# Last token tile turned between the value products, layer 1 in whole tiles, and a last batch normalised and stored tile by tile

## The chip, the core and the metric

The kernel runs on one core of one Trainium2 chip. A core has TensorE (matrix products into PSUM), VectorE, ScalarE, GpSimd and SyncE (SP), which issues most of the transfers. The metric is the device time of one execution in microseconds.

## What is computed

Eight batches of 512 tokens with 256 features go through one attention block with a layer norm, a second layer norm of the sum with the input, a feed-forward part of three layers with ternary weights, and a last layer norm:

```python
# attention: 16 heads of 16, softmax over keys, then multiplied by triu
p = softmax(q @ k.T / sqrt(512)) * triu
x1 = layernorm(x + p @ v) * gamma + beta
x2 = layernorm(x + x1)
# feed-forward, hidden size 1024
h = silu((x2 @ w1) * s1) * ((x2 @ w2) * s2)
h = gelu((h @ h1) * s1h)
h = gelu((h @ h2) * s2h)
out = layernorm(x2 + (h @ w3) * s3)
```

All inputs and outputs are float32.

## The kernel before, in words

The order of each engine's work is written out by hand, one instruction stream per engine, with counting semaphores between them. `after(engine, s, b, n, count)` makes an engine wait until semaphore s has had n signals for each earlier batch and `count` in this one. A loop runs over the batches; in each come the attention of the batch, the head of its feed-forward part (together with the projections of the next batch's q, k and v), and the feed-forward part.

Tokens are in four tiles of 128 (QT = 4), features in two (DT = 2), the hidden size in eight (HT = 8). VectorE normalises one token tile for each group of four heads: `first_norm` and `second_norm`. The power -0.5 of the variance is computed by GpSimd (`rstd`), so each norm goes from VectorE to GpSimd and back. The normalised x2 (tile `X`) is turned by TensorE (`turn_x2`, a transpose by 128 x 128 blocks), in two parts: part 0 is the token tiles 0 to 2 (384 tokens, PSUM banks 4 and 5), part 1 is token tile 3 (128 tokens, bank 0). Each part is then taken by ScalarE into a rounded `X2hi` (`take_x2_hi`), and VectorE computes the rest into `X2lo` (`split_x2`), so that a product of layer 1 is one with the high and one with the low part, both at the rate of the rounded type.

Layer 1 has for each hidden tile m a gate product (`which` 0) and an up product (`which` 1), each of 2 (feature tiles) x 2 (high, low) instructions. `bank1` gives their PSUM bank. ScalarE computes the gate (L639), VectorE the product `hidA_full` (L861) and its rounded part `hidA_hi` (L865), GpSimd the rest `hidA_lo` (`low_part`, L487). Hidden tiles 0 and 1 are computed by `first_layer` (L1173) in two pieces of 384 and 128 tokens, so that they can begin before part 1 is turned; tiles 2 to 7 are computed in `feed_forward` (L1078) over 512 tokens at once. Layer 2 begins on TensorE right behind layer 1 and takes `hidA_lo` tile by tile.

Between the two turns TensorE does work of the next batch: the k projections (L909) and the value products (`project_v`, L926, 16 instructions for the four token tiles). In the last batch there is no next one, and `keep_warm` puts filler products there (L972), whose result is not used. In the other batches the first scores of the next batch are computed inside layers 2 and 3 (L964), from stacks that SP loads from a scratch tensor once GpSimd's `qk_lo` (L507) has been stored.

At the end of a batch VectorE takes y tile by tile (`add_y`: L810, L812, L814), and `last_norm` computes the four aggregates, one add of epsilon, GpSimd one power over four columns (`rstd_last`), and VectorE four normalised tiles into `OUT`, which SP stores with one transfer of 512 KB (L446, in the last batch L468). The order of the head on TensorE before:

```python
turn_x2(b, 0, last)
if not last:
    project(b + 1, range(DT, 2 * DT))
    project_v(b + 1, range(QT))
else:
    keep_warm(7, 20)
first_layer(b, last, 0, 0)
turn_x2(b, 1, last)
first_layer(b, last, 1, 0)
first_layer(b, last, 0, 1)
first_layer(b, last, 1, 1)
```

There is a second, `general`, branch of the feed-forward part for weights that the rounded type doesn't hold; with these inputs it isn't taken.

Of the kernel before, what the change touches and what calls it, by code (L numbers as in the profile page):

```python
# [10 lines left out]
ALU = mybir.AluOpType  # L11
# [42 lines left out]
def build_program(nc, x, xT, wqT, wkT, wvT, bqk, bv, gamma, beta, w1T, w2T, h1T, h2T, scales,  # L54
# [101 lines left out]
    with ExitStack() as ctx:  # L156
# [82 lines left out]

        def bank1(m, which):  # L240

            return 4 + (2 * m + 2 + which) % 4

# [4 lines left out]
        def bank_y(t):  # L248

            return 4 + (t + 2) % 4  # L250
# [42 lines left out]
        def _(sp):  # L293
# [171 lines left out]
            with sp.Else():  # L465
                from_first_feed_forward(False)
            sp.wait_ge(out_ready, QT * B)
            sp.dma_start(out[(B - 1) * S:B * S, :].rearrange("(t p) d -> p t d", p=P), OUT[:]).then_inc(out_stored, 16)  # L468
            sp.wait_ge(out_stored, 16 * B)
            sp.wait_ge(rows_stored, 4 * 16 * B)  # L470
# [4 lines left out]
        def _(pool):  # L475
# [69 lines left out]
            def body(b, first, last):  # L545
                after(pool, probs_ready, b, STEPS, 0)
                after(pool, range_known, b, 1, 1)
                nc.gpsimd.memset(GRANT[:, 1:2], 0.0)
                unbounded = pool.value_load(UNBOUNDED[0:1, 0:1], min_val=0, max_val=1)
                with pool.If(unbounded):  # L550
                    attention(b, first, False)
                with pool.Else():
                    attention(b, first, True)
                if not last:
                    split_qk(b + 1, range(0, 1))
                rstd(b, QT - 1, 0)
                rstd(b, QT - 1, 1)
                if not last:
                    after(pool, x2_ready, b, QT, QT)
                    split_qk(b + 1, range(1, 2 * DT))  # L560
                for m in range(HT):
                    low_part(0, b, hidA_full, hidA_hif, hidA_lo, m)
                for m in range(HT):
                    low_part(HT, b, hidC_full, hidC_hif, hidC_lo, m)
                for m in range(HT):
                    low_part(2 * HT, b, hidA_full, hidA_hif, hidA_lo, m)
                if last:
                    rstd_last(b)

# [9 lines left out]
        def _(act):  # L579
# [37 lines left out]
            def body(b, first, last):  # L617
# [17 lines left out]
                for m in range(HT):  # L635
                    after(act, ffn1, b, 2 * HT, 2 * m + 1)
                    if m >= 2:
                        after(act, up_done, b, HT, m - 1)
                    nc.scalar.activation(SIL[:, m % 2, :], PS[:, bank1(m, 0), :], ACT.Silu,  # L639
                                         scale=SC[:, 0, m:m + 1]).then_inc(gate_done, 1)  # L640
                    if m < 2 * DT and not last:
                        square_qk(b + 1, m)
# [31 lines left out]
        def _(dve):  # L674
# [87 lines left out]

            def first_norm(b, t):

                n = t * N_TILE
                after(dve, z_taken, b, NQUAD, t + 1)
                if t == 0:
# [8 lines left out]
                nc.vector.scalar_tensor_tensor(out=Z[:, t, :], in0=Z[:, t, :], scalar=MV[:, t, 0:1], in1=GAM[:],  # L776
                                               op0=ALU.subtract, op1=ALU.mult).then_inc(norm_step, 1)
                after(dve, beta_added, b, QT, t + 1)
                after(dve, norm_step, b, N12, n + 5)
# [15 lines left out]

            def split_x2(b):

                for part in range(2):
                    after(dve, x2_hi_done, b, 2, part + 1)
                    src, dst = x2_part(part)  # L800
                    nc.vector.tensor_tensor(X2lo[:, :, dst], src, X2hif[:, :, dst], ALU.subtract).then_inc(x2_split, 1)

            def add_y(b, tiles, back=0):

                for t in tiles:
                    if t == 0:
                        after(dve, x2_ready, b, QT, QT)
                        after(dve, out_stored, b, 16, 0)
                    after(dve, y_done, b, QT, t + 1 - QT * back)
                    nc.vector.tensor_tensor(T1[:, t, :], PS[:, bank_y(t), 0:D], S3[:], ALU.mult).then_inc(y_taken, 1)  # L810
                    after(dve, y_taken, b, QT, t + 1 - QT * back)
                    nc.vector.tensor_tensor(X[:, t, :], X[:, t, :], T1[:, t, :], ALU.add).then_inc(last_step, 1)  # L812
                    after(dve, last_step, b, N_LAST, 2 * t + 1 - N_LAST * back)
                    nc.vector.bn_stats(STAT[:, t, :], X[:, t, :]).then_inc(last_step, 1)  # L814

            def last_norm(b, parts=range(3)):
# [13 lines left out]

            def attention(b, first):

                if not first:
                    last_norm(b)
                for g in range(NQUAD):
# [6 lines left out]
                    take_z(b, g)  # L842
                    first_norm(b, g)
                    second_norm(b, g)

            def body(b, first, last):
                attention(b, first)
                split_x2(b)
                if not last:
                    take_v(b + 1)  # L850

                for m in range(HT):
# [5 lines left out]
                    if m == 4 and not last:  # L858
                        sum_squares(b + 1)
                        after(dve, rows_stored, b, 4 * 16, 8 * 16)  # L860
                    nc.vector.scalar_tensor_tensor(out=hidA_full[:, m, :], in0=PS[:, bank1(m, 1), :],  # L861
                                                   scalar=SC[:, 1, m:m + 1], in1=SIL[:, m % 2, :],
# [5 lines left out]
                for layer, full, hi in ((2, hidC_full, hidC_hi), (3, hidA_full, hidA_hi)):  # L868
                    for m in range(HT):
# [7 lines left out]
                        nc.vector.tensor_copy(hi[:, m, :], full[:, m, :]).then_inc(hi_done, 1)  # L877
                add_y(b, range(QT - 1))
                if last:
                    last_norm(B)  # L880

# [18 lines left out]
        def _(pe):  # L900
# [145 lines left out]
            def feed_forward(b, last, general):  # L1046
# [39 lines left out]

                for m in range(0 if general else 2, HT):
                    for which, w in ((0, W1), (1, W2)):
# [4 lines left out]
                        if m >= 2:  # L1093
                            after(pe, (gate_done, up_done)[which], b, HT, m - 1)
                        product(PS[:, bank1(m, which), :], DT, lambda k: w[:, k, m * P:(m + 1) * P],
                                lambda k: (X2hi[:, k, :], X2lo[:, k, :], X2hif[:, k, :], X2lof[:, k, :]),
# [67 lines left out]
            def first_layer(b, last, m, part):  # L1164
# [5 lines left out]
                for which, w in ((0, W1), (1, W2)):  # L1170
                    for k in range(DT):
                        for d in (X2hi, X2lo):
                            ins = nc.tensor.matmul(PS[:, bank1(m, which), tokens], w[:, k, m * P:(m + 1) * P],  # L1173
                                                   d[:, k, tokens], start=(k == 0 and d is X2hi),
                                                   stop=(k == DT - 1 and d is X2lo), skip_group_check=True)
# [3 lines left out]
            def next_projections(b, last, general):  # L1179
# [3 lines left out]
                if not last:  # L1183
                    project(b + 1, range(DT, 2 * DT))
                    project_v(b + 1, range(QT))
                else:
                    keep_warm(7, 20)
                if not general:
                    first_layer(b, last, 0, 0)
                turn_x2(b, 1, last)  # L1190
                if not general:
                    first_layer(b, last, 1, 0)
                    first_layer(b, last, 0, 1)
                    first_layer(b, last, 1, 1)

# [68 lines left out]
```

## Time and profile before

| | |
|---|---|
| median of 3 runs | 1227.19 us (1227.16 to 1228.64) |
| profiled execution | 1228.32 us |
| its span, first to last instruction | 1226.6 us |
| TensorE busy | 1176.1 us, 96% |
| VectorE busy | 781.1 us, 64% |
| ScalarE busy | 503.6 us, 41% |
| GpSimd busy | 561.6 us, 46% |
| mean granted TensorE clock | 0.972 of full speed |

Times of the profile are counted from the first instruction; busy shares are means over stages that differ. In the profile's names PE is TensorE, PEld its weight loads, DVE VectorE, ACT ScalarE, POOL GpSimd and SPq the queue of SP. A row of the timeline gives start and duration, and in brackets how long the engine was idle before it and what released it. Products are pipelined: their shown durations overlap, and the time that a product takes from the chain is the distance between two starts.

### The profile page before, as it was taken

The numbers are of one execution on the slowest core, as the hardware profiler recorded it, in microseconds if no ns is written. First come the engines' busy times: TensorE is split into PE (matmuls) and PEld (weight loads), VectorE is DVE, ScalarE is ACT, GpSimd is POOL, SyncE is SP. The second block draws the span as 40 slices with busy tenths as digits, with TensorE's granted clock in tenths as the row PEclk, the third lists the DMA queues.
The fourth block names the chain that finished last, engine by engine and source line by source line (L and its number), as shares of the span: only waits on it lengthen the run. The fifth ranks groups of instructions, "written<-read, shape, count | busy, mean of one in ns | idle before, by whom it ended". The sixth has DMA issues, their size and how long they took to land.

```text
span 1226.6 us, 18621 instructions
## 1 busy us (share of the span) xinstructions
PE 1176.1 (96%) x7446; PEld 819.2 (67%) x7446; DVE 781.1 (64%) x1135; ACT 503.6 (41%) x676; POOL 561.6 (46%) x502
## 2 busy tenths in 40 slices
PE   5589999999999999999999999999999999999997
PEld 3244777657775677757777587756778577775886
DVE  3937666578646786477664786466864777748412
ACT  5366411664127621475116641276213751155310
POOL 4347522565236642376224652356423752246432
PEclk8569999999999999999999999999999999999999
DMA  8951322413234222233214132342222432141000
GB/s 297 339 150 52 123 71 72 113 48 114 68 77 105 106 67 71 62 97 138 71 49 117 53 121 64 86 106 93 80 71 53 106 138 70 37 104 37 1 1 18
DMA packets 44845, 111.74 MB, mean 91 GB/s; under 512 B 7952, under 2 KB 19600, under 8 KB 44688
## 3 DMA queue, kind: packets, MB, share of 16 engines
q1 hardware_dynamic: 40576, 98.68, 28.0%
q10 hardware_dynamic: 4176, 11.80, 2.8%
q8 instruction: 61, 1.00, 0.3%
q14 instruction: 32, 0.26, 0.1%
HBM read 88.95 MB, written 21.50 MB: 90 GB/s over the span
## 4 chain that ended last, share of the span: by engine, by line
PE 86%; DMA 4%; issue 3%; POOL 3%; DVE 3%; SPq 1%; ACT 0%; POOLq 0%; DVEq 0%; ACTq 0%
PE PS L1078 51%; PE PS L995 9%; PE PS L964 6%; PE PS L1014 5%; PE PS L909 4%; PE PS L1173 3%; PE PS L1021 2%; PE PS L926 2%; PE PS L1027 2%; DVE neg_max L722 2%; POOL diag_probs L500 1%; DMA max_rows_d<-max_rows 1%; DMA s_b<-s_dram 1%; DMA x_tok<-x_dram 1%; POOL rstd L513 1%
## 5 line engine op out<-in xcount | busy, mean ns | idle before, releaser
L714 DVE TENSOR_REDUCE neg_max<-PS 128x3 f32<-128x1536 f32 x168 | 257.6, 1575 | 61.2 <-PE PS L964 61.2
L487 POOL TENSOR_TENSOR hidA_lo<-hidA_full,hidA_hi 128x512 fp32r<-128x512 f32 x128 | 174.2, 1361 | 244.6 <-DVE hidA_hi L877 186.7
L623 ACT ACTIVATE probsT<-PS 128x1024 f32<-128x1024 f32 x256 | 248.1, 1021 | 83.3 <-PE PS L995 83.3
L1078 PE MATMUL PS<-hidA_hi,g 128*128 128x512 f32 x512 | 205.6, 402 | 0.0
L1078 PE MATMUL PS<-hidC_hi,g 128*128 128x512 f32 x512 | 203.9, 398 | 0.0
L1078 PE MATMUL PS<-hidA_lo,g 128*128 128x512 f32 x512 | 200.0, 391 | 0.0
L1078 PE MATMUL PS<-hidC_lo,g 128*128 128x512 f32 x512 | 199.8, 390 | 0.0
L500 POOL TENSOR_TENSOR diag_probs<-probsT,mask 128x512 f32<-128x512 f32 x120 | 156.8, 1311 | 59.8 <-PE PS L1078 31.1
L487 POOL TENSOR_TENSOR hidC_lo<-hidC_full,hidC_hi 128x512 fp32r<-128x512 f32 x64 | 82.4, 1288 | 194.4 <-DVE hidC_hi L877 194.4
L995 PE MATMUL PS<-stacks 66*128 66x512 f32 x512 | 154.6, 424 | 5.6 <-DMA stacks<-max_rows_d 5.4
L646 ACT ACTIVATE hidC_full<-PS,scales 128x512 f32<-128x512 f32 x64 | 44.2, 690 | 239.4 <-PE PS L1078 239.4
L646 ACT ACTIVATE hidA_full<-PS,scales 128x512 f32<-128x512 f32 x64 | 44.1, 689 | 224.9 <-PE PS L1078 224.9
L1078 PEld LDWEIGHTS PS<-hidA_hi,g 128*128 128x128 f32 x512 | 96.5, 188 | 37.1 <-issue 15.4
L1078 PEld LDWEIGHTS PS<-hidC_hi,g 128*128 128x128 f32 x512 | 96.1, 188 | 32.3 <-issue 12.8
L995 PEld LDWEIGHTS PS<-stacks 66*128 66x128 f32 x512 | 86.5, 192 | 44.5 <-issue 21.3
L1078 PEld LDWEIGHTS PS<-hidC_lo,g 128*128 128x128 f32 x512 | 96.2, 188 | 19.0
L1078 PEld LDWEIGHTS PS<-hidA_lo,g 128*128 128x128 f32 x512 | 96.3, 188 | 18.4
L964 PE MATMUL PS<-stacks 64*128 64x512 f32 x480 | 83.9, 448 | 18.6 <-issue 11.8
L1014 PE MATMUL PS<-probsT,ones_col 128*32 128x512 f32 (+3 forms) x1024 | 96.3, 448 | 4.9 <-issue 2.6
L877 DVE CAST hidA_hi<-hidA_full 128x512 fp32r<-128x512 f32 x64 | 27.3, 427 | 107.5 <-ACT hidA_full L646 107.5
L964 PEld LDWEIGHTS PS<-stacks 64*128 64x128 f32 x480 | 39.8, 193 | 55.4 <-issue 23.9
L1078 PE MATMUL PS<-x2T_hi,w 128*128 128x512 f32 x192 | 75.2, 392 | 0.0
(114 smaller groups left out, 1734.8 us busy)
## 6 DMA issues: line engine op xcount, KB each, us to landing
stacks<-qk_rows SPq DMA_DIRECT2D x124, 256.0 KB
stacks<-qk_rows SPq DMA_DIRECT2D x248, 128.0 KB
qk_rows<-qk_hi SPq DMA_DIRECT2D x16, 512.0 KB, 2.7
qk_rows<-qk_lo SPq DMA_DIRECT2D x16, 512.0 KB, 2.8
xT_sb<-xT_dram SPq DMA_DIRECT2D x8, 512.0 KB, 4.2
g_raw<-h1T_dram ACTq DMA_DIRECT2D x4, 1024.0 KB, 12.4
g_raw<-h2T_dram ACTq DMA_DIRECT2D x4, 1024.0 KB, 16.8
x_tok<-x_dram SPq DMA_DIRECT2D x8, 512.0 KB, 5.5
```

The costliest lines, as they stand in the source:

```text
L487: nc.gpsimd.tensor_tensor(lo[:, m, :], full[:, m, :], hi[:, m, :], ALU.subtract).then_inc(lo_done, 1)
L500: nc.gpsimd.tensor_tensor(masked(s), PT[:, s % RING, :, kt * P:(kt + 1) * P], MASK[:].rearrange("p (a m) -> p a m", a=1).to_broadcast([P, ...
L623: nc.scalar.activation(PT[:, s % RING, 2 * pair:2 * pair + 2, :], PS[:, 2 * pair:2 * pair + 2, :], ACT.Exp, scale=SCALE).then_inc(exp_done, 1)
L646: nc.scalar.activation(full[:, m, :], PS[:, bank23(m), :], ACT.Gelu, scale=SC[:, layer, m:m + 1]).then_inc(gelu_done, 1)
L714: nc.vector.tensor_reduce(NEGM[:, group // 2, at + lo:at + hi], PS[:, 3 * side:3 * side + hi - lo, :], AX.X, ALU.max, negate=True).then_in ...
L877: nc.vector.tensor_copy(hi[:, m, :], full[:, m, :]).then_inc(hi_done, 1)
L909: ins = nc.tensor.matmul(PS[:, bank_qk(n), :], w[:, k, c * P:(c + 1) * P], XT[:, k, :], start=(k == 0), stop=(k == DT - 1))
L964: ins = nc.tensor.matmul(PS[:, base + apart * side + n, :], stack(pair)[rows, qt * P:(qt + 1) * P], stack(2 + pair)[rows, :], start=True, ...
L995: ins = nc.tensor.matmul(PS[:, j, :], ST[0:ROWS, g % 2, 1, j, kt * P:(kt + 1) * P], ST[0:ROWS, g % 2, 0, j, :], start=True, stop=True)
L1014: nc.tensor.matmul(PS[32 * j:32 * j + 32, bank, lo:S], ONE[:, 0:32], PT[:, s % RING, j, lo:S], start=(kt == 0), stop=False, skip_group_che ...
L1078: ins = nc.tensor.matmul(out, d if swapped else w, w if swapped else d, start=(k == 0 and part == 0), stop=(k == kts - 1 and part == 1))
L1173: ins = nc.tensor.matmul(PS[:, bank1(m, which), tokens], w[:, k, m * P:(m + 1) * P], d[:, k, tokens], start=(k == 0 and d is X2hi), stop=( ...
```

## The change

In batches 0 to 6 the turn of the last token tile (part 1) moves from behind the first piece of layer 1 to between the first and the second half of the value products. Layer 1 then has no pieces of 384 and 128 tokens: all eight hidden tiles are computed by `feed_forward` over 512 tokens.

In the last batch the pieces stay, and a third hidden tile is computed in two pieces, in banks 2 and 3. Filler products are 13 instead of 20, and the pieces of 384 tokens of hidden tiles 0 and 1 stand ahead of the turn of part 1. The split of part 0 on VectorE moves into the first norm of the last token tile, ahead of its wait for GpSimd's power. The last norm is done by `final_norm`, with aggregate, epsilon, a power of one column and the normalised tile for each token tile; SP stores each token tile by itself (128 KB).

```diff
         def bank1(m, which, last=False):
+            if last and m == 2:
+                return 2 + which
             return 4 + (2 * m + 2 + which) % 4
...
-            sp.wait_ge(out_ready, QT * B)
-            sp.dma_start(out[(B - 1) * S:B * S, :].rearrange("(t p) d -> p t d", p=P), OUT[:]).then_inc(out_stored, 16)
-            sp.wait_ge(out_stored, 16 * B)
+            for t in range(QT):
+                sp.wait_ge(out_ready, QT * (B - 1) + t + 1)
+                sp.dma_start(out[(B - 1) * S + t * P:(B - 1) * S + (t + 1) * P, :], OUT[:, t, :]).then_inc(out_stored, 16)
+            sp.wait_ge(out_stored, 16 * (B - 1 + QT))
...
                 if last:
-                    rstd_last(b)
+                    for t in range(QT):
+                        after(pool, last_step, b, N_LAST, 4 * t + 4)
+                        nc.gpsimd.tensor_tensor(NY[:, t:t + 1], VE[:, t:t + 1], HALF[:, t:t + 1],
+                                                ALU.pow).then_inc(rstd_last_done, 1)
...
                 nc.vector.scalar_tensor_tensor(out=Z[:, t, :], in0=Z[:, t, :], scalar=MV[:, t, 0:1], in1=GAM[:],
                                                op0=ALU.subtract, op1=ALU.mult).then_inc(norm_step, 1)
+                if split_first:
+                    split_x2(b, 0)
                 after(dve, beta_added, b, QT, t + 1)
...
+            def final_norm(b):
+
+                def out(t):
+                    after(dve, rstd_last_done, b, 1, t + 1)
+                    normalize(X, OUT, t).then_inc(out_ready, 1)
+
+                for t in range(QT):
+                    n = 4 * t
+                    if t == 0:
+                        after(dve, x2_ready, b, QT, QT)
+                        after(dve, out_stored, b, 16, 0)
+                    after(dve, y_done, b, QT, t + 1)
+                    nc.vector.tensor_tensor(T1[:, t, :], PS[:, bank_y(t), 0:D], S3[:], ALU.mult).then_inc(y_taken, 1)
+                    after(dve, y_taken, b, QT, t + 1)
+                    nc.vector.tensor_tensor(X[:, t, :], X[:, t, :], T1[:, t, :], ALU.add).then_inc(last_step, 1)
+                    after(dve, last_step, b, N_LAST, n + 1)
+                    nc.vector.bn_stats(STAT[:, t, :], X[:, t, :]).then_inc(last_step, 1)
+                    after(dve, last_step, b, N_LAST, n + 2)
+                    nc.vector.bn_aggr(MV[:, t, :], STAT[:, t, :]).then_inc(last_step, 1)
+                    after(dve, last_step, b, N_LAST, n + 3)
+                    nc.vector.tensor_scalar(VE[:, t:t + 1], MV[:, t, 1:2], EPS, None, ALU.add).then_inc(last_step, 1)
+                    if t == 1:
+                        out(0)
+                for t in range(1, QT):
+                    out(t)
...
-                for m in range(0 if general else 2, HT):
+                for m in range(3 if last and not general else 0, HT):
...
                 if not last:
                     project(b + 1, range(DT, 2 * DT))
-                    project_v(b + 1, range(QT))
+                    project_v(b + 1, range(QT // 2))
+                    turn_x2(b, 1, last)
+                    project_v(b + 1, range(QT // 2, QT))
                 else:
-                    keep_warm(7, 20)
-                if not general:
-                    first_layer(b, last, 0, 0)
-                turn_x2(b, 1, last)
-                if not general:
-                    first_layer(b, last, 1, 0)
-                    first_layer(b, last, 0, 1)
-                    first_layer(b, last, 1, 1)
+                    keep_warm(7, 13)
+                    if not general:
+                        first_layer(b, last, 0, 0)
+                        first_layer(b, last, 1, 0)
+                    turn_x2(b, 1, last)
+                    if not general:
+                        after(pe, exp_done, b, 2 * STEPS, 2 * STEPS)
+                        first_layer(b, last, 2, 0)
+                        for m in range(3):
+                            first_layer(b, last, m, 1)
```

## Rows read from the trace of the kernel before

**Rows 1.** Page, part 4: the chain that ended last, by engine.

```profile
PE 86%; DMA 4%; issue 3%; POOL 3%; DVE 3%; SPq 1%; ACT 0%; POOLq 0%; DVEq 0%; ACTq 0%
```

**Rows 2.** Chain in order of time, batch 6: start us, us, what.

```profile
990.32 3.45 PE PS L926 x16
993.77 1.39 PE PS L1173 x8
...
995.38 3.13 PE PS L1173 x24
```

**Rows 3.** Timeline, batch 6: start, us, engine, line, operation [idle before <-releaser].

```profile
990.97 0.41 DVE L760 TENSOR_SCALAR x_tok<-x_tok,mean_var,rstd 128x256 f32<-128x256 f32 x1 [0.67 <-POOL rstd L513]
...
991.46 3.74 POOL L507 TENSOR_TENSOR qk_lo<-qk_full,qk_hi 128x512 fp32r<-128x512 f32 x3 [0.53 <-DVE x_tok L760]
...
995.83 0.42 DVE L801 TENSOR_TENSOR x2T_lo<-PS,x2T_hi 128x256 fp32r<-128x256 f32 x1 [3.58 <-ACT x2T_hi L584]
...
997.90 0.51 SPq L306 DMA_DIRECT2D stacks<-qk_rows  x1
997.93 0.76 DVE L861 SCALAR_TENSOR_TENSOR hidA_full<-PS,scales,gate 128x512 f32<-128x512 f32 x1 [0.54 <-ACT gate L639]
```

**Rows 4.** Timeline, batch 6, start of layer 2.

```profile
1010.30 0.74 DVE L861 SCALAR_TENSOR_TENSOR hidA_full<-PS,scales,gate 128x512 f32<-128x512 f32 x1
...
1012.11 1.29 POOL L487 TENSOR_TENSOR hidA_lo<-hidA_full,hidA_hi 128x512 fp32r<-128x512 f32 x1 [0.36 <-DVE hidA_hi L865]
...
1013.60 0.40 PE L1078 MATMUL PS<-hidA_hi,g 128*128 128x512 f32 x1
```

**Rows 5.** Timeline, last batch: norm of the last tile, filler products.

```profile
1130.14 4.80 PE L972 MATMUL PS<-w 128*128 128x512 f32 x20
...
1130.42 0.81 ACT L584 ACTIVATE x2T_hi<-PS 128x768 fp32r<-128x768 f32 x1 [6.03 <-PE PS L1043]
...
1131.45 0.48 DVE L776 SCALAR_TENSOR_TENSOR z<-z,mean_var,gamma_b 128x256 f32<-128x256 f32 x1
...
1132.47 0.48 DVE L781 SCALAR_TENSOR_TENSOR x_tok<-z,rstd,x_plus_beta 128x256 f32<-128x256 f32 x1 [0.54 <-POOL rstd L513]
1132.99 0.43 DVE L788 BATCH_NORM_STATS2 stats<-x_tok 128x6 f32<-128x256 f32 x1
...
1134.48 0.41 DVE L760 TENSOR_SCALAR x_tok<-x_tok,mean_var,rstd 128x256 f32<-128x256 f32 x1 [0.66 <-POOL rstd L513]
```

**Rows 6.** Chain in order of time, last batch, head of layer 1.

```profile
1134.90 0.88 DVE x2T_lo L801
...
1135.82 1.66 PE PS L1173 x8
...
1137.70 3.13 PE PS L1173 x24
1140.83 69.00 PE PS L1078 x304
```

**Rows 7.** Timeline, last batch, VectorE and GpSimd in layer 1.

```profile
1140.25 0.75 DVE L861 SCALAR_TENSOR_TENSOR hidA_full<-PS,scales,gate 128x512 f32<-128x512 f32 x1 [1.67 <-ACT gate L639]
...
1143.04 0.74 DVE L861 SCALAR_TENSOR_TENSOR hidA_full<-PS,scales,gate 128x512 f32<-128x512 f32 x1
...
1144.70 0.74 DVE L861 SCALAR_TENSOR_TENSOR hidA_full<-PS,scales,gate 128x512 f32<-128x512 f32 x1
...
1144.86 1.28 POOL L487 TENSOR_TENSOR hidA_lo<-hidA_full,hidA_hi 128x512 fp32r<-128x512 f32 x1 [0.36 <-DVE hidA_hi L865]
```

**Rows 8.** Timeline, the end.

```profile
1218.70 0.42 DVE L810 TENSOR_TENSOR scaled_y<-PS,s_b 128x256 f32<-128x256 f32 x1 [0.57 <-PE PS L1078]
...
1223.20 0.38 SPq L468 DMA_DIRECT2D out_dram<-out_tok  x1
```

**Rows 9.** The last 512 KB store: us from issue to landing.

```profile
DMA to landing us min/median/max: 2.9/2.9/2.9
```

**Rows 10.** DMA issues: line, queue, count, KB each, median us to landing.

```profile
max_rows_d<-max_rows SPq DMA_DIRECT2D x16, 32.0 KB, 1.5
```

More of the change, by code:

```diff
@@ L237, in build_program, with bank1 @@
         GUARD_AT = {2: 0, 5: 1}
-        def bank1(m, which):
+        def bank1(m, which, last=False):
+            if last and m == 2:
+                return 2 + which
             return 4 + (2 * m + 2 + which) % 4
@@ L638, in body @@
                         after(act, up_done, b, HT, m - 1)
-                    nc.scalar.activation(SIL[:, m % 2, :], PS[:, bank1(m, 0), :], ACT.Silu,
+                    nc.scalar.activation(SIL[:, m % 2, :], PS[:, bank1(m, 0, last), :], ACT.Silu,
                                          scale=SC[:, 0, m:m + 1]).then_inc(gate_done, 1)
@@ L761, in normalize, with first_norm @@
                                                ALU.subtract, ALU.mult)
[L763 removed]
+            def first_norm(b, t, split_first=False):
                 n = t * N_TILE
@@ L794, in second_norm, with split_x2 @@
                 normalize(X, X, t).then_inc(x2_ready, 1)
[L796 to L801, printed above, removed]
+            def split_x2(b, part):
+                after(dve, x2_hi_done, b, 2, part + 1)
+                src, dst = x2_part(part)
+                nc.vector.tensor_tensor(X2lo[:, :, dst], src, X2hif[:, :, dst], ALU.subtract).then_inc(x2_split, 1)
             def add_y(b, tiles, back=0):
@@ L829, in last_norm, with attention @@
                         normalize(X, OUT, t).then_inc(out_ready, 1)
-            def attention(b, first):
+            def attention(b, first, last):
                 if not first:
@@ L842, in attention @@
                     take_z(b, g)
-                    first_norm(b, g)
+                    first_norm(b, g, last and g == NQUAD - 1)
                     second_norm(b, g)
             def body(b, first, last):
-                attention(b, first)
-                split_x2(b)
+                attention(b, first, last)
+                if not last:
+                    split_x2(b, 0)
+                split_x2(b, 1)
                 if not last:
@@ L860, in body @@
                         after(dve, rows_stored, b, 4 * 16, 8 * 16)
-                    nc.vector.scalar_tensor_tensor(out=hidA_full[:, m, :], in0=PS[:, bank1(m, 1), :],
+                    nc.vector.scalar_tensor_tensor(out=hidA_full[:, m, :], in0=PS[:, bank1(m, 1, last), :],
                                                    scalar=SC[:, 1, m:m + 1], in1=SIL[:, m % 2, :],
@@ L877, in body @@
                         nc.vector.tensor_copy(hi[:, m, :], full[:, m, :]).then_inc(hi_done, 1)
-                add_y(b, range(QT - 1))
                 if last:
-                    last_norm(B)
+                    final_norm(b)
+                else:
+                    add_y(b, range(QT - 1))
             dve.wait_ge(consts_in, 16 * N_CONSTS)
@@ L1094, in feed_forward @@
                             after(pe, (gate_done, up_done)[which], b, HT, m - 1)
-                        product(PS[:, bank1(m, which), :], DT, lambda k: w[:, k, m * P:(m + 1) * P],
+                        product(PS[:, bank1(m, which, last), :], DT, lambda k: w[:, k, m * P:(m + 1) * P],
                                 lambda k: (X2hi[:, k, :], X2lo[:, k, :], X2hif[:, k, :], X2lof[:, k, :]),
@@ L1172, in first_layer @@
                         for d in (X2hi, X2lo):
-                            ins = nc.tensor.matmul(PS[:, bank1(m, which), tokens], w[:, k, m * P:(m + 1) * P],
+                            ins = nc.tensor.matmul(PS[:, bank1(m, which, last), tokens], w[:, k, m * P:(m + 1) * P],
                                                    d[:, k, tokens], start=(k == 0 and d is X2hi),
```

## The prediction

> **What bounds the kernel now.** I read the page's chain of work first, then that chain in order of time around each place that the diff touches, then the timeline of the other engines there, and last the issues and landings of the transfers. TensorE carries 86% of the chain [rows 1], so what shortens a stretch in which TensorE runs without a gap comes off the end, and what only moves work of the other engines does not. Three stretches matter. In batch 6 (batches 1 to 5 repeat it to 0.1 us, batch 0 has the same products) TensorE goes straight from the 16 value products into the products of layer 1, the two transposes of the last token tile and again layer 1, with no wait: 3.45, 1.39, 0.22 and 3.13 us [rows 2]. In the last batch the same products stand behind the chain norm, x2T_lo, first product [rows 5, 6]. At the end TensorE is through at about 1218.7, and 8 us of VectorE, GpSimd and one store follow [rows 8].
>
> **Batches 0 to 6: whole tiles.** Removed are 16 products of 384 columns and 16 of 128 (two hidden tiles, two weights, two halves of the inner dimension, high and low part). They take 1.39 us for eight of 384 columns, so 0.174 each, and together with the rest 1.39 + 3.13 = 4.52 us [rows 2]; the 16 narrow ones are then 4.52 - 16 x 0.174 = 1.74 us, 0.109 each. Added are 16 products of 512 columns, at 69.00/304 = 0.227 us each [rows 6], 3.63 us. That is 0.89 us less in each of seven batches, 6.2 us, if the turn between the value products waits for nothing. The cover that held the turn before (the 1.39 us of layer 1 ahead of it, and 1.39 us behind it) is gone, so both sides of it are worked out:
> - Ahead of it: eight value products end at 990.32 + 1.73 = 992.05. The token tile that the turn reads is normalised at 990.97 + 0.41 = 991.38 [rows 3]. The margin is 0.67 us. Behind this wait stand, on TensorE, everything, and on the other engines the split of part 1.
> - Behind it: the turn ends at 992.27. Before, it ended at 995.38 and the low part was there at 995.83 + 0.42 = 996.25 [rows 2, 3], so 0.87 us later; that gives 993.14 now. VectorE and ScalarE are free by then. The eight remaining value products last to 994.00, a margin of 0.86 us. Nothing waits.
>
> What is next late is the far end of layer 1. VectorE writes the last hidden tile at 1010.30, GpSimd has its low part at 1012.11 + 1.29 = 1013.40, and the product that needs it starts at 1013.60: only 0.2 us to spare, because VectorE is behind TensorE there [rows 4]. The product will now start 0.89 us earlier. But VectorE's run starts earlier too: its first tile (997.93 before [rows 3], behind the split, the bias of v and a load of ScalarE's table) can start once the first two groups of whole-tile products are through, 994.00 + 1.82 = 995.8, about 2 us earlier. It waits there for qk_lo as well, which GpSimd ends at 991.46 + 3.74 = 995.20 [rows 3]. So I take no stall; the bound is what is left if VectorE won nothing, 0.89 - 0.2 = 0.7 us a batch, 4.8 us in all. The row loads for the next batch hang on qk_lo's store and not on TensorE; they start at 997.90 [rows 3] and the first unit of scores needs them at 1010.4 instead of 1011.2, 12 us after the issue. No cost. No transfer is added or moved here.
>
> The Trainium skill ("TensorE: Matmul & The Clock Gate", section "Wait — 56ns, not 53.3ns?") gives start to start N/2.4 GHz plus 2.5 ns for any width. By it a 384 and a 128 column product cost 0.163 + 0.056 us against 0.216 for 512, so that whole tiles would give nothing. This trace disagrees for the narrow ones (0.109 us, [rows 2]); the sum by that page would be 4.1 us instead of 10.3.
>
> **Last batch, head.** The split of part 0 moves from behind the norm of the last tile into it. Its input from ScalarE is there at 1130.42 + 0.81 = 1131.23; it starts behind the gamma step, 1131.45 + 0.48 = 1131.93, and takes 0.88 us of the chain [rows 5, 6], to 1132.85 with the small overlap of neighbours on VectorE. GpSimd's power is done by 1132.4, so the next step starts 0.40 us later than its 1132.47, and the tile is ready at 1134.89 + 0.40 = 1135.3. TensorE's filler products are cut from 20 to 13. The 20 begin at 1130.14 and take 0.227 each, so 13 end at 1133.1, after the split. There the first product starts, not at 1135.82 [rows 6]. Two groups of eight at 384 columns go to 1135.9, then the turn (its tile was ready at 1135.3, margin 0.6), 0.22 us, then eight more for hidden tile 2, 1.39, and 24 narrow ones, 24 x 0.109 = 2.62: tiles 0 to 2 are through at 1140.1. Before it was 1140.83 plus one tile of 1.82, 1142.65. The 384 + 128 split of the third tile is in this (8 x 0.056 = 0.45 us dearer). The gain at this point is about 2.4 us (2.2 to 2.5).
>
> Part of it is given back: here nothing keeps VectorE ahead. From the turn's end to VectorE's first hidden tile took 1140.25 - 1137.70 = 2.55 us (the split of part 1, a table load, the first gate) [rows 6, 7]. From there to the eighth tile it needs at its own pace 1143.04 - 1140.25 + 5 x 1.66 = 11.1 us, and the low part is there 3.1 us after a tile starts (1144.86 + 1.28 - 1143.04) [rows 7]: 16.75 us after the turn. TensorE wants it after 1.39 + 2.62 + 5 x 1.82 + 14 x 0.227 = 16.3 us. Stall 0.5 us, between 0 (VectorE's casts are 0.43 where GpSimd is idle and up to 0.97 where it runs) and 1.0. Net for the head: 2.4 - 0.5 = 1.9 us, from 1.4 to 2.4.
>
> **Last batch, tail.** All four aggregates, one add, one power over 4 columns and four norms stood behind the last tile's statistics; now a tile has its own. The last y is taken at 1218.70; VectorE may be 0.2 us late, since the norm of tile 0 (0.41) is put ahead of tile 2. Two steps of 0.46 lead to the statistics at 1219.8. From statistics to the normalised tile took 1134.48 + 0.41 - 1132.99 = 1.90 us in the layer norm of one tile, its power of GpSimd included [rows 5], and the norms of tiles 1 and 2 (0.35 each) fit in the power's time. So the last tile is out at 1221.7; before, all were at 1223.2 [rows 8]. That is 1.5 us. SP then issues four stores of 128 KB for one of 512 KB, the first far ahead, two in the 0.8 us before the last; an issue was 0.38 us, so they follow one another without delaying the last by more than 0.1. The single store landed 2.9 us after its issue; a 32 KB store takes 1.5 [rows 9, 10]. A 128 KB store lies between; with its two neighbours in flight I take 2.1, so 0.8 us less. Tail: 2.2 us, from 1.3 to 2.8.
>
> For the last store "DMA: Bandwidth & Descriptors" of the Trainium skill (section "Anatomy of one DMA — SWDGE (gpsimd) path") has a fixed 2.0 us plus bytes over 436 GB/s: 2.3 us against 3.2, an estimate of 0.9 us less where I have 0.8, and a warning that four stores have four fixed parts; only the last one's is on the path.
>
> **Sum.** 6.2 + 1.9 + 2.2 = 10.3 us. The profiled execution took 1228.32 us (span 1226.6), so 1218.0 for one like it; the median of the runs is 1227.19, 1.1 below it, and gives 1216.9.
>
> **Rivals.**
> - *The far end of layer 1 eats the gain.* VectorE and GpSimd arrive when they did before, and TensorE waits ahead of layer 2. For it: the 0.2 us margin [rows 4]. Against it: VectorE starts 2 us earlier. At 0.7 us a batch the time is 1216.9 + 4.8 = 1221.7; half of it 1219.3.
> - *Slower: the turn is late.* The norm of the last tile ends behind the eighth value product, and all of TensorE stands. A wait of 0.67 us hides; beyond this it costs one for one, and only when the tile is over 0.67 + 10.3/7 = 2.1 us late does the kernel get slower. At 3 us late a batch: 1216.9 + 7 x 2.3 = 1233. Against it: six batches agree to 0.1 us, and the change puts nothing ahead of this norm except in the last batch.
> - *Narrow products cost what their columns do*, by that page: the whole-tile edit is worth nothing, 1223.1. The rows speak against it.
> - *Tail and head give only their lower bounds*, a store that lands after 2.9 us and a 1.0 us stall: 1216.9 + 0.9 + 0.5 = 1218.3.
> - *More than I see*: no stall, the store after 1.5 us: 1216.9 - 0.5 - 0.6 = 1215.8.
>
> **How the numbers follow.** Three gains as worked out (1215.8 to 1218.3): 0.76. Layer 1's far end takes a part (1218.3 to 1222): 0.13. No gain from whole tiles (about 1223): 0.02. The turn is late by little, still faster (1222 to 1224.7): 0.03. About no change: 0.02; slower: 0.02. A still larger gain (down to 1214.5), from a wait that goes with the earlier starts: 0.02. The likeliest is 1216.9. The range 1215.0 to 1221.0 leaves out the upper cases and little else. 0.2% is 2.5 us here, about what a measurement of this kernel can tell from no change: faster 0.96, same 0.02, slower 0.02.
>
> **What the profile after would show.** In batches 0 to 6: two transposes between two groups of eight value products, no 384 or 128 column products, no wait on x2T_lo or x_tok, and layer 2 starting 0.9 us earlier behind the first value product. VectorE's first hidden tile 5.5 us behind that product's start instead of 7.6. In the last batch: first product of layer 1 at most 0.3 us behind x2T_lo, and a wait of TensorE on hidA_lo early in layer 2 of about 0.5 us. At the end: a power of one column 2 us ahead of the last store, whose issue to landing is 2.1 us. A wait ahead of the turn, or on hidA_lo in batches 0 to 6, would make the prediction wrong.

## The result, and the profile after

The changed kernel took 1218.64 us (median of 5 runs, 1216.89 to 1221.79) against 1227.19 before; the ratio is 0.9929, with a 95% interval from 0.9911 to 0.9948. Measured once more beside three experiments it took 1217.58 against 1228.51, ratio 0.9918 [0.9894, 0.9943]. The profiled execution took 1220.53 us, with a span of 1218.8. I had said 1216.9, in a range from 1215.0 to 1221.0.

The page of the profile after, the chain by engine, which is as it was [rows 1].

```profile
PE 86%; DMA 4%; POOL 3%; issue 3%; DVE 3%; SPq 1%; ACT 0%; POOLq 0%; ACTq 0%; DVEq 0%
```

The chain in order of time around the second turn of batch 6, which answers to [rows 2]:

```profile
988.51 1.73 PE PS L962 x8
990.24 0.22 PE PS L1079 x2
990.46 1.73 PE PS L962 x8
992.19 16.37 PE PS L1114 x72
```

Eight value products, the turn, eight value products, layer 1, with no wait between them. And the timeline of the same batch, which answers to [rows 3, 4]:

```profile
989.17 0.41 DVE L766 TENSOR_SCALAR x_tok<-x_tok,mean_var,rstd 128x256 f32<-128x256 f32 x1 [0.67 <-POOL rstd L516]
...
990.91 0.42 DVE L808 TENSOR_TENSOR x2T_lo<-PS,x2T_hi 128x256 fp32r<-128x256 f32 x1 [0.46 <-ACT x2T_hi L590]
...
994.14 0.75 DVE L896 SCALAR_TENSOR_TENSOR hidA_full<-PS,scales,gate 128x512 f32<-128x512 f32 x1 [0.69 <-PE PS L1114]
...
1008.75 1.28 POOL L490 TENSOR_TENSOR hidA_lo<-hidA_full,hidA_hi 128x512 fp32r<-128x512 f32 x1 [0.36 <-DVE hidA_hi L900]
...
1010.88 0.39 PE L1114 MATMUL PS<-hidA_hi,g 128*128 128x512 f32 x1
```

The token tile is ready at 989.17 + 0.41 = 989.58, the turn starts at 990.24: the margin is 0.66 us, where 0.67 was forecast. The low part is there at 991.33, 0.86 us ahead of layer 1. VectorE's first hidden tile starts at 994.14, 5.6 us behind the first value product (7.6 before). At the far end GpSimd's last low part is ready at 1010.03 and used at 1010.88: the margin has grown from 0.2 to 0.85 us.

The head of the last batch, first its chain (answers to [rows 6]), then TensorE's wait there:

```profile
1126.73 2.99 PE PS L1008 x13
1129.72 2.80 PE PS L1209 x16
1132.53 0.22 PE PS L1079 x2
1132.74 4.02 PE PS L1209 x32
1136.77 4.63 PE PS L1114 x20
...
1148.17 1.29 POOL hidA_lo L490
...
1149.50 10.72 PE PS L1114 x46
```

```profile
PE PS L1114 <- POOL hidA_lo L490: 0.4, 1, 0.4
```

Layer 1 goes from the filler products straight on; then the chain leaves TensorE, and comes back to it by way of GpSimd's last `hidA_lo`. The wait is shown as 0.4 us, but the product that waited started at 1149.50 on the chain, where 1148.9 was due (layer 2 began at 1125.86 + 19.89 = 1145.75, and 14 products of 0.227 us stand ahead of it). So the stall is 0.4 to 0.6 us. And the end (answers to [rows 8, 9]):

```profile
1213.54 0.42 DVE L835 TENSOR_TENSOR scaled_y<-PS,s_b 128x256 f32<-128x256 f32 x1
...
1215.21 1.25 DVE L766 TENSOR_SCALAR out_tok<-x_tok,mean_var,rstd 128x256 f32<-128x256 f32 x3
```

Then SP's own timeline, and the summary of the landings of the last batch's three stores (line 471), in two fences:

```profile
1215.64 1.32 SPq L471 DMA_DIRECT2D out_dram<-out_tok  x3
```

```profile
DMA to landing us min/median/max: 1.7/1.8/1.8
```

The last tile is out at 1216.46, 2.92 us after VectorE begins to take the last y (4.48 before), and its store, the last of the three, lands 1.8 us after its issue (2.9 before).

**Where the time went.** Two tables worked out from the timelines. First, the steps, counted from the first value product of a batch (batches 0 to 6), from the first transpose (last batch), and from the start of VectorE's instruction that takes the last y:

| us | before | after |
|---|---|---|
| first value product to layer 2 | 19.15 to 19.18 | 18.19 to 18.23 |
| first value product to the first values of attention | 101.07 to 101.11 | 100.10 to 100.13 |
| last batch: first transpose to layer 2 | 22.11 | 19.89 |
| last batch: first transpose to the first gelu | 25.94 | 24.42 |
| last y to last tile out | 4.48 | 2.92 |
| last issue to landing | 2.9 | 1.8 |

That is 7 x 0.96 + 1.5 + 1.6 + 1.1 = 10.9 us, but the spans differ by 7.8. Second, the distance from a batch's first value product to the next batch's:

| batch | 0 | 1 | 2 | 3 | 4 | 5 |
|---|---|---|---|---|---|---|
| before | 144.82 | 143.46 | 143.40 | 143.45 | 144.34 | 143.40 |
| after | 142.48 | 143.15 | 143.48 | 142.57 | 143.66 | 143.19 |

The shortest distances differ by 0.92, close to what the steps say. But after the change four of six batches lie 0.7 to 1.2 us above the shortest; before it two did, by 0.9 and 1.4. Such batches are called late here. Together with the last attention (0.9 late before, not late after) all that lies above the shortest is 3.4 us before and 3.7 after. The rest stands ahead of all edits: the first value product of batch 0 comes at 129.82 instead of 127.28 (1.5 of the 2.5 us is TensorE's one wait for the stacks at the start, 6.9 us for 5.4; TensorE's granted clock also stood at its lower level, 1.2 GHz, until 87.6 us there and until 81.5 before, with 3.4 us more at 122.5, and what that adds was not separated). -10.9 + 0.3 + 2.5 = -8.1, so 0.3 us stay unassigned. So two things had to be asked of the chip: whether the three edits are worth what they seem, each by itself, and what makes a batch late.

### The profile page after: what moved, and what is told of

It reads as the page before. It is cut to its first block, busy times and chain, and to the rows that moved or that the text cites. A ratio compares the mean times of both kernels' runs of the same rounds, so it can differ in the third digit from the quotient of the medians.

```text
span 1218.8 us, 18416 instructions
## 1 busy us (share of the span) xinstructions
PE 1167.4 (96%) x7335; PEld 807.9 (66%) x7335; DVE 772.8 (63%) x1138; ACT 505.9 (42%) x676; POOL 562.9 (46%) x505
## 4 chain that ended last, share of the span: by engine, by line
PE 86%; DMA 4%; POOL 3%; issue 3%; DVE 3%; SPq 1%; ACT 0%; POOLq 0%; ACTq 0%; DVEq 0%
PE PS L1114 53%; PE PS L1031 9%; PE PS L1000 6%; PE PS L1050 5%; PE PS L945 4%; PE PS L1057 3%; PE PS L962 2%; PE PS L1063 2%; DVE neg_max L728 2%; POOL diag_probs L503 2%; DMA max_rows_d<-max_rows 1%; DMA s_b<-s_dram 1%; DMA x_tok<-x_dram 1%; POOL rstd L516 1%; PE PS L1079 1%
## 5 line engine op out<-in xcount | busy, mean ns | idle before, releaser
L503 POOL TENSOR_TENSOR diag_probs<-probsT,mask 128x512 f32<-128x512 f32 x120 | 157.0, 1313 | 61.3 <-PE PS L1114 31.1
L1114 PE MATMUL PS<-x2T_hi,w 128*128 128x512 f32 x244 | 96.4, 395 | 0.0
L1114 PE MATMUL PS<-x2T_lo,w 128*128 128x512 f32 x244 | 95.0, 390 | 0.0
```

Source lines behind the costliest of these rows:

```text
L503: nc.gpsimd.tensor_tensor(masked(s), PT[:, s % RING, :, kt * P:(kt + 1) * P], MASK[:].rearrange("p (a m) -> p a m", a=1).to_broadcast([P, ...
L1114: ins = nc.tensor.matmul(out, d if swapped else w, w if swapped else d, start=(k == 0 and part == 0), stop=(k == kts - 1 and part == 1))
```

## The experiments

**Each edit by itself.** The kernel before with one of the three edits. The first, batches 0 to 6 only:

```diff
                 if not last:
                     project(b + 1, range(DT, 2 * DT))
-                    project_v(b + 1, range(QT))
+                    project_v(b + 1, range(QT // 2))
+                    turn_x2(b, 1, last)
+                    project_v(b + 1, range(QT // 2, QT))
+                    return
...
-                for m in range(0 if general else 2, HT):
+                for m in range(2 if last and not general else 0, HT):
```

> The kernel before with the edit of batches 0 to 6 alone: turn of the last token tile between the halves of the value products, layer 1 in whole tiles; head and tail of the last batch as before. My theory: from the first value product to layer 2 each of the seven batches is 0.9 to 1.0 us shorter, all of it reaches the end but for what the landing of the x load adds or takes by chance, so 6.2 to 6.8 us less, 1220.7 us. Rival (the far end of layer 1 gives it back): a wait on hidA_lo in each batch, 1 to 3 us less. Rival (attention gives back a part, since it is paced by a transfer and not by TensorE): 3 to 5 us less.

The second has only the diff's lines for the last batch's head, the third only those for its tail.

> The kernel before with the head of the last batch alone (split of part 0 inside the norm, 13 filler products, three hidden tiles in pieces). My theory: 2.2 us less at the start of layer 2, of which about 0.5 us is given back by a wait on hidA_lo, so 1.7 to 1.9 us less, 1225.4 us. Rival (VectorE's pace decides layer 1 wholly): 1 us or less.

> The kernel before with the tail of the last batch alone (norm, power and store for each token tile). My theory: 1.5 us less to the last normalised tile and 0.8 to 1.2 less from the last issue to its landing, 2.3 to 2.7 us less, 1224.7 us. Rival (four stores cost more than one): 1.5 us less or under.

| edit | median, us | beside it, before | ratio [95%] |
|---|---|---|---|
| batches 0 to 6 | 1223.34 | 1228.52 | 0.9958 [0.9943, 0.9973] |
| head | 1227.09 | 1228.52 | 0.9984 [0.9969, 0.9999] |
| tail | 1227.21 | 1228.52 | 0.9982 [0.9970, 0.9995] |

The ratios make 5.2, 2.0 and 2.2 us, with intervals of 2 us to either side, and add to 9.4. The traces are sharper. With the first edit alone, value product to layer 2 is 18.20 to 18.23 in all seven batches, and there is no wait on hidA_lo at layer 2's start. With the head alone, first transpose to layer 2 is 19.87 and to the first gelu 24.41; with the tail alone, 2.93 us lead from the last y to the last tile, and the last store lands after 1.8. Each edit does in its place what it does in the changed kernel; none depends on another.

**The turn moved, the tiles still in pieces.**

```diff
-                    project_v(b + 1, range(QT))
+                    project_v(b + 1, range(QT // 2))
+                    turn_x2(b, 1, last)
+                    project_v(b + 1, range(QT // 2, QT))
                 else:
                     keep_warm(7, 20)
                 if not general:
                     first_layer(b, last, 0, 0)
-                turn_x2(b, 1, last)
+                if last:
+                    turn_x2(b, 1, last)
```

> The turn of batches 0 to 6 between the value products, but hidden tiles 0 and 1 still in pieces of 384 and 128 tokens: the move without the whole tiles. My theory: the narrow pieces cost what they did, 0.109 us each, and the turn is hidden in either place, so no change (within 0.5 us of before, 1227.2). Rival (narrow products cost what their columns do and the gain comes from the place of the turn): as e1_whole.

Ratio 0.9999 [0.9987, 1.0011]. The chain of batch 6:

```profile
991.32 1.73 PE PS L926 x8
993.04 0.22 PE PS L1043 x2
993.26 1.73 PE PS L926 x8
994.99 4.52 PE PS L1173 x32
```

The 32 products in pieces take 4.52 us here as they did before, where 16 whole ones take 3.64 (16.37/72 each). The place of the turn is worth nothing by itself; it only makes the whole tiles possible. The trace of before also shows where a product stops getting cheaper. From one start to the next, in the median, it takes 0.227 us at 512 columns, 0.174 at 384, 0.120 at 256 (the products of y) and 0.111 at 128: halving 256 columns saves 0.01 us. Every one of these products has a weight load of its own, and in layer 1's pieces the loads never follow each other by less than 0.108 us. That the weight load sets the price of the narrow products is what these figures suggest; no run tests it.

**The turn ahead of all value products.**

```diff
-                    project_v(b + 1, range(QT // 2))
                     turn_x2(b, 1, last)
-                    project_v(b + 1, range(QT // 2, QT))
+                    project_v(b + 1, range(QT))
```

> The changed kernel, with the turn of the last token tile ahead of all 16 value products instead of between their halves. My theory: the tile is normalised 1.06 us behind the start of the value products, so TensorE stands for about 1.1 us in batches 1 to 6 (not in batch 0), 6 to 7 us above the changed kernel; layer 1 itself as in the changed kernel. It tells how near the turn stands to being late: 0.67 us from its place. Rival (the wait is hidden): no change.

1225.59 us, 0.9973 [0.9956, 0.9989] of before, 7 to 8 us above the changed kernel's two medians. Its waits:

```profile
PE PS L1079 <- DVE x_tok L766: 7.3, 6, 1.2
```

Six waits of 1.2 us, one in each of batches 1 to 6. This is the wait that the slower rival names. With the turn 1.73 us earlier on TensorE, the waits take back what the edit of these batches gains (7.3 us against some 6.7); that the time still stays below the kernel before can be put down to head and tail.

**The last batch's rounding on ScalarE.** VectorE keeps the product with the gate, ScalarE rounds.

```diff
+            def round_hidden(b, m):
+                after(act, up_done, b, HT, m + 1)
+                nc.scalar.activation(hidA_hi[:, m, :], hidA_full[:, m, :], ACT.Identity).then_inc(hi_done, 1)
...
+                    if last and m:
+                        round_hidden(b, m - 1)
+                if last:
+                    round_hidden(b, HT - 1)
...
-                    after(dve, up_done, b, HT, m + 1)
-                    nc.vector.tensor_copy(hidA_hi[:, m, :], hidA_full[:, m, :]).then_inc(hi_done, 1)
+                    if not last:
+                        after(dve, up_done, b, HT, m + 1)
+                        nc.vector.tensor_copy(hidA_hi[:, m, :], hidA_full[:, m, :]).then_inc(hi_done, 1)
```

> The changed kernel, with the rounding of the hidden tiles of layer 1 in the last batch on ScalarE instead of VectorE. My theory: VectorE's pace of 1.66 us a tile behind a late start is what TensorE waits for on hidA_lo ahead of layer 2's first tile; with 0.75 us a tile VectorE follows TensorE, the wait of 0.5 us is gone and layer 2's first tile ends that much earlier. Rival (GpSimd's 1.3 us a tile sets it): the wait stays.

It ran only once, in 1215.95 us, and that time alone shows nothing; the trace does. The wait of TensorE on hidA_lo ahead of the end of layer 2's first tile is gone, and first transpose to the first gelu is 23.81 us, against 24.42 in the changed kernel. So 0.61 us is what VectorE's pace gives back in the head.

**What makes a batch late: the x load.** In the attention, VectorE adds x to z of the first token tile (L775), and GpSimd adds beta to x (L543), behind a product with the mask (L503). Both additions wait for the load of x. A late batch (2) of the changed kernel, and below it the same batch where it was not late (the kernel with the first edit alone, lines 769 and 540):

```profile
528.17 0.74 POOL L543 TENSOR_TENSOR x_plus_beta<-x_tok,beta_b 128x256 f32<-128x256 f32 x1 [0.27 <-DMA x_tok<-x_dram]
...
528.20 1.00 DVE L775 TENSOR_TENSOR z<-z,x_tok 128x256 f32<-128x256 f32 x1 [2.35 <-DMA x_tok<-x_dram]
```

```profile
526.72 0.71 DVE L769 TENSOR_TENSOR z<-z,x_tok 128x256 f32<-128x256 f32 x1 [1.64 <-DMA x_tok<-x_dram]
...
527.11 0.93 POOL L540 TENSOR_TENSOR x_plus_beta<-x_tok,beta_b 128x256 f32<-128x256 f32 x1
```

Counted from the batch's first value product, GpSimd's product ends at 112.4 to 112.5 us in every batch of the changed kernel. When x lands after 112.3, GpSimd's addition starts some 0.03 us ahead of VectorE's, and VectorE's ends 0.3 us behind it, 1.1 us after the landing. When x lands earlier, VectorE's add starts first, between 111.5 and 112.4, and ends at 112.7 to 112.8 wherever it starts: beside GpSimd's product it takes up to 1.20 us, and ends 0.3 us behind that. So landings from 111.4 to 112.3 are all worth the same, and one behind that costs 0.7 us at once and then its own delay. I first took the place of the load in SP's queue for the cause, and moved it ahead of the stacks of the third head group:

```diff
                 load_stacks(b, 1, True)
-                load_stacks(b, 2, True)
-
                 after(sp, out_ready, b, QT, 0)
                 sp.dma_start(X[:], x[...]).then_inc(x_in, 16)
-                if True:
-                    sp.dma_start(out[...], OUT[:]).then_inc(out_stored, 16)
+                load_stacks(b, 2, True)
+                sp.dma_start(out[...], OUT[:]).then_inc(out_stored, 16)
                 load_stacks(b, 3, True)
```

> The changed kernel, with SP issuing the x load and the store of the previous output ahead, not behind, the seven loads of the third head group's stacks (the store right behind those loads). My theory: in the attention the landing of x sets when GpSimd can go on, so an x load issued some 2 us earlier takes 1 to 2 us off each of seven batches; 7 to 14 us below the changed kernel's 1219, about 1209. Rival (attention is paced by TensorE or the masks anyway): no change. Rival (the stacks of the third group now come late): slower, a wait of TensorE on stacks.

1257.27 us, ratio 1.0232 [1.0205, 1.0260]. The last rival holds:

```profile
PE PS L1029 <- DMA stacks<-max_rows_d: 30.2, 8, 7.7
```

The changed kernel has one such wait, of 6.9 us, at the start. The x load started only 0.4 us sooner (106.47 us after the first value product instead of 106.88), since it waits for `out_ready`, and not for the queue; behind that wait SP held the stacks back, and TensorE stood for them in each of the seven later attentions, six times for 2.6 to 2.9 us and once for 7.7. At six of these seven waits the granted clock fell to 1.2 GHz, for 3.4 to 13.7 us, 51 us in all. At the seventh (2.6 us) it stayed at 2.4 GHz, and that batch's distance is 144.97 us; the others are 146.75 to 154.36. So the waits themselves, 24 us, are some three fifths of the 39 us lost. What an earlier x is worth this run doesn't tell; the last experiment with it does. Next, the store of the previous output moved behind the fourth group's stacks:

```diff
                 sp.dma_start(X[:], x[...]).then_inc(x_in, 16)
-                if True:
-                    sp.dma_start(out[...], OUT[:]).then_inc(out_stored, 16)
                 load_stacks(b, 3, True)
+                sp.dma_start(out[...], OUT[:]).then_inc(out_stored, 16)
```

> The changed kernel, with the store of the previous output issued behind the loads of the fourth group's stacks instead of right behind the x load. Theory (the store's 512 KB compete with the x load, and this makes the landing of x differ by up to 1 us from batch to batch): x lands 0.3 to 1 us earlier and evenly, 2 to 7 us less. Rival (the spread comes from elsewhere): no change.

And, the other way, ahead of the x load:

```diff
+                sp.dma_start(out[...], OUT[:]).then_inc(out_stored, 16)
                 sp.dma_start(X[:], x[...]).then_inc(x_in, 16)
-                if True:
-                    sp.dma_start(out[...], OUT[:]).then_inc(out_stored, 16)
                 load_stacks(b, 3, True)
```

> The changed kernel, with the store of the previous output issued ahead of the x load instead of behind it, so that x lands later. My theory: x lands about 0.5 us later at least, every batch is a late one, each interval 0.7 us and more above 142.45; 3 to 10 us above the changed kernel. Rival (the spread doesn't come from x's landing): no change.

With the store later: 1216.60 us, 0.9904 [0.9885, 0.9923], not to be told from the changed kernel; two of six batches are late, and the median landing of x is 5.0 instead of 5.2 us. Inconclusive. With the store first: 1225.68, 0.9972 [0.9958, 0.9985]; x lands after 112.4 us in every batch, and all six are late, 143.50 to 144.29. At last x in two transfers, the first token tile by itself:

```diff
+            def load_x(b):
+                sp.dma_start(X[:, 0, :], x[b * S:b * S + P, :]).then_inc(x0_in, 16)
+                sp.dma_start(X[:, 1:QT, :], x[...]).then_inc(x_in, 16)
...
-                        after(pool, x_in, b, 16, 16)
+                        after(pool, x_in if t else x0_in, b, 16, 16)
...
-                if t == 0:
-                    after(dve, x_in, b, 16, 16)
+                if t < 2:
+                    after(dve, x_in if t else x0_in, b, 16, 16)
```

> The changed kernel again, unedited, beside the next three on one chip. My theory: from one batch's value products to the next takes 142.45 us where VectorE's add of x to z starts before GpSimd's addition of beta, and 0.6 to 1.2 us more where x lands so late that both start together; how many batches of the six are late is chance (4 in the first profile, 2 in other kernels with the same edit). So here 0 to 6 late ones, and a median 8 to 11 us below the kernel before.

> The changed kernel, with x loaded by two transfers: the first token tile (128 KB) by itself, then the other three. VectorE's and GpSimd's first use of x wait for the small one alone. My theory (the spread of the batches is the landing of x against the time at which GpSimd is free): the small load lands 1 us and more earlier, no batch is late, all six intervals are 142.4 to 142.6 us, and the median is 1 to 4 us below the changed kernel's. Rival (the spread is the engines' own): late batches as before. Rival (two transfers land later than one): more late batches, slower.

| kernel, batch | VectorE's add ends | to the next batch | difference |
|---|---|---|---|
| before, 5 | 113.68 | 143.40 | 29.72 |
| before, 4 | 114.62 | 144.34 | 29.72 |
| changed, again, 1 | 112.73 | 142.49 | 29.76 |
| changed, 1 | 113.41 | 143.15 | 29.74 |
| changed, 2 | 113.75 | 143.48 | 29.73 |
| store first, 0 | 114.24 | 144.00 | 29.76 |
| x in two, 2 | 112.70 | 142.46 | 29.76 |
| x in two, 0 | 110.83 | 142.29 | 31.46 |

(All from the batch's first value product.) From the end of that add to the next batch is 29.7 to 29.8 us in every kernel in which TensorE has no other wait in between (with the turn first it is 31.4, with the x load early 33 to 40), until the add is so early that something else decides. With x in two transfers the six distances are 142.29 to 142.46, none late, and the time is 1214.27 us, 0.9885 [0.9862, 0.9908]; the changed kernel beside it had three late ones and 1217.58 (0.9918 [0.9894, 0.9943], so the two intervals overlap a little). The adds that ended 1.4 to 1.9 us before 112.7 made a distance shorter by only 0.2 us: an earlier x removes late batches and gains next to nothing beyond that, so my first theory of 1 to 2 us a batch was wrong.

**Both together.** x in two transfers, and the last batch's rounding on ScalarE.

> The kernel of the x load in two transfers and the rounding of the last batch's first hidden layer on ScalarE together. My theory: the gains add, 0.5 us below the kernel with the x load in two transfers. Rival: no difference to it, since 0.5 us is under what the runs can tell; the wait on hidA_lo ahead of layer 2 is gone in the trace in any case.

1214.51 us, 0.9884 [0.9862, 0.9907]: no difference to x in two transfers that runs can show. Its six distances are 142.26 to 142.49, none late. In its trace the wait on hidA_lo is gone (23.81 to the first gelu), and its span of 1211.6 is the shortest of all. Its median is the lower by 3 us against the changed kernel beside it, with intervals that overlap a little.

## Why the prediction was right

- *Whole tiles, 6.2 us.* Right in mechanism, a little small: 0.95 to 0.98 us a batch up to the attention, 6.7 in all, where I had 0.89. The narrow products do cost 0.11 us each: the pieces were 4.52 us again with the turn moved. By the rule of the Trainium skill ("TensorE: Matmul & The Clock Gate", section "Wait — 56ns, not 53.3ns?") pieces and whole tiles would cost the same; the trace disagrees by 0.9 us in 16 products, and the run with whole tiles alone has 0.9958 of the time before. That rule is given for products back to back and reckons no weight load, while here each product has one.
- *The turn waits for nothing.* Right: margins 0.66 and 0.86 us, where I had 0.67 and 0.86. Moved up by 1.73 us it waits 1.2 in six batches.
- *No stall at the far end of layer 1.* Right, and by more than I claimed: the margin grew from 0.2 to 0.85.
- *Head, 1.9 us.* Measured 1.5: 2.22 to layer 2 where I had 2.4, and 0.6 to 0.7 given back where I had 0.5. The cause of what is given back was the one named, VectorE's pace: with its rounding elsewhere 0.61 us come back.
- *Tail, 2.2 us.* Measured 2.7. The last tile is 1.56 sooner (1.5 forecast), and the last 128 KB store lands after 1.8 us, where I took 2.1. The formula of "DMA: Bandwidth & Descriptors" in the Trainium skill (section "Anatomy of one DMA — SWDGE (gpsimd) path") gives an estimate of 2.3 us; it is a fit of transfers that GpSimd issues, these are issued by SP, and the trace is below it.
- *The sum, 10.3 us.* The steps make 10.9, 8.6 arrived in the median of the first runs, 10.9 in those beside the experiments (1228.51 - 1217.58). What the sum had left out is that in the attention a transfer decides by chance: I noted the x load nowhere, though the chain of before holds it. The weak step is "what shortens a stretch in which TensorE runs without a gap comes off the end": it does, on the mean, but in each batch 0.7 to 1.4 us can be added by the landing of x. The changed kernel had 4 and 3 late batches of six in its two profiles, two other kernels with the same edit and the same transfers 2 each. Whether the change makes late batches likelier is open. With the last attention counted too, 8 of 28 are late in the four profiles with batches 0 to 6 unedited and 11 of 28 in these four, and GpSimd is free 5.6 us after the x load's issue in both (107.83 to 113.39, and 106.88 to 112.44). Not all of it is chance, either: in each of the four unedited profiles batch 0 is the latest, and its load is issued 0.4 to 0.8 us behind the usual 107.83. The 2.5 us ahead of batch 0's first value product also differ between executions (127.3 to 129.8 over the profiles with unchanged code there), and are no part of the change. That 1218.64 lies in the range owes something to the range's width: the upper part was meant for a loss in layer 1, and late batches and a late start fell into it.

## What to carry to other kernels

A product over few columns with weights of its own costs more than its share of the columns (here 128 columns cost nearly what 256 do): cut a tile in pieces only where the wait that it fills is longer than the pieces' extra, and look first for other work to fill it. When TensorE is the bound and a stage gets shorter, ask which transfer lands next to a point where two engines both wait for it: there the same code gives distances that differ by 1 us, and a small load of its own for the first tile took the late batches away (none in the 12 distances of two kernels). Landing it earlier still gained almost nothing. Before an instruction is moved up in a queue, see what it waits for: its wait moves with it, and holds back all that was ahead of it.

## What the runs showed of the hardware

- VectorE's add of 128 x 256 elements took 0.42 us alone, 1.00 when it started just behind GpSimd's addition, and up to 1.54 when it ran beside one of GpSimd's products of 128 x 512 (the kernel with x in two transfers, batch 2). In either case it ended 0.3 us behind the instruction of GpSimd that had started before it.
- From start to start, products that each load weights of 128 columns took 0.227 us at 512 columns, 0.174 at 384, 0.120 at 256 and 0.111 at 128.
- A store of 128 KB landed 1.7 to 1.8 us after its issue with up to three in flight, one of 512 KB with none beside it after 2.9; in the changed kernel the load of 512 KB beside a store took 5.2 us in the median, 4.5 to 5.9.
- With the x load early, waits of TensorE of 2.6 to 2.9 us were followed by 3.4 to 13.7 us at a granted clock of 1.2 GHz in five cases and by none in a sixth; waits of 1.2 us (the turn first) by none in six.
- With one unchanged beginning, the first value product came between 127.3 and 129.8 us. A difference of 2 us between two profiles is no proof of a change.
